# Filling the attention stacks in two halves of eight heads, each half with a semaphore of its own

## The chip, the cores and the metric

The kernel runs on one core of one Trainium2 chip. The metric is the device time of one execution in microseconds (us); the time of a kernel is the median of its runs. Five engines work side by side, each on a list of instructions of its own that it takes strictly in order: PE (matrix products), DVE (element-wise work and reductions), ACT (activations), POOL (element-wise work, memsets), and SP, which here only issues the copies that the DMA engines carry out. They wait for each other through semaphores.

## The reference

Four small transformer layers in a row, on a batch of 4 with 256 tokens of 128 channels and 16 heads. Layer 0 has heads of 64 channels, layer 1 is a graph attention over 20 nodes, layers 2 and 3 have heads of 8 channels. The attentions of layers 2 and 3 are what the change touches:

```python
# layer 2
energy = jnp.einsum('bhqd,bhkd->bhqk', q, k)
att = jax.nn.softmax(energy, axis=-1) / D ** 0.5
out = jnp.einsum('bhqk,bhkd->bhqd', att, v)
...
# layer 3
scores = jnp.einsum('bhqd,bhkd->bhqk', q, k) * scale
scores = jnp.where(causal, scores, -jnp.inf)
attn = jax.nn.softmax(scores, axis=-1)
out = jnp.einsum('bhqk,bhkd->bhqd', attn, v)
```

## The kernel before

Every batch element goes through the layers by itself, and the phases of different elements are interleaved. `schedule()` lays out once, when the program is built, which phase gets the next tick; `walk` then writes each engine's instructions in that order. So the order on every engine is fixed, and an engine that waits holds up everything behind it.

There are twelve attentions, four in each of the layers 0, 2 and 3. This document writes (2, 3) for layer 2, batch element 3. An attention has 16 heads. For a head PE first makes plain scores (`scores`, L1433 in layer 2, L1437 and L1439 in layer 3), DVE takes row maxima from them (L1131, L1128), these are turned by PE (L1462), copied by ACT (L953) and spread by POOL (L767), and six steps after the plain scores PE makes the transposed scores (`scores_t`, L1479 and L1481). ACT takes their exponentials (L961) and PE multiplies them with the values (`values`, L1527). The tail of one attention overlaps the head of the next.

In layers 2 and 3 a query or a key of 8 channels is split into three bf16 parts. PE multiplies the queries' and keys' projections (`qkv`, L1707), ACT and DVE split them (L1039, L1336, L1045, L852), and for one attention SP writes six blocks of 64 KB into the DRAM tensor `scratch` (L721). From there copies fill the *stack*: 72 rows of queries and 72 rows of keys for each head, so that one product of 72 rows forms all nine products of parts. There are two rooms for stacks, `b % ROOMS`; the rooms are slices of the tensor `big`. One fill is six copies of 192 KB:

- three copies for the queries (L731), each the three-fold repetition of one part over 24 rows, 8 KB in a row;
- three copies for the keys (L736), each all three parts over 24 rows, 8 KB in a row.

A fill of room r for the third and later attentions of these layers may begin only when the attention that used the room two before has made its 16th transposed scores (L727, semaphore `st_full`). For the first two, where layer 0 used the room, the copies wait for memsets by POOL (`stack_zero`). All copies of all fills count on one semaphore, `stack_ready`; PE waits once, ahead of an attention's first plain scores, until it shows that all six copies of its fill have landed (L1543). SP also waits for it before it overwrites `scratch` (L717).

Of the kernel before, what the change touches and what calls it, by code (L numbers as in the profile page):

```python
# [14 lines left out]
B, T, D = 4, 256, 128  # L15
ROOMS = 2
H_ROOMS = 3
NT = T // 128
H = 16
DH0 = 64  # L20
DH = D // H
# [51 lines left out]
PARTS = 3  # L73
COPIES = PARTS * DH
# [13 lines left out]
ATTENTIONS = [(layer, b) for layer in (0, 2, 3) for b in range(B)]  # L88
# [30 lines left out]
U_BASE = {a: H * n for n, a in enumerate(ATTENTIONS)}  # L119
# [124 lines left out]
def score_heads(layer, i):  # L244

    if layer != 0:
        return [i] if i < H else []
    return [i, i + 1] if i < H and i % 2 == 0 else []
# [10 lines left out]
def mT_step(layer, i):  # L259

    return next((g for g in range(GROUPS) if mT_step_of(layer, g) == i), None)
# [18 lines left out]
def x_after(*phase):  # L280
    return X_UPDATES.index(phase) + 1
# [102 lines left out]
def cond_seq_kernel(nc, x_t, adj, w0, wqk0, w1, w2, w3, wp2, wproj3, vecs, rows, out_t):  # L384
    with ExitStack() as ctx:
# [3 lines left out]
        def sem(name):  # L389
            return ctx.enter_context(nc.semaphore(name))  # L390
# [37 lines left out]
        stacks = big[:, :, :].bitcast(BF16).rearrange("p r (s h t) -> p r s h t", s=2, h=H)  # L428
# [47 lines left out]
        scratch = nc.dram_tensor("scratch", [ROOMS, 2, PARTS, DH, H * T], BF16).ap()  # L476
# [25 lines left out]
        with nc.Block() as block:  # L502
            @block.sync
            def _(sp):

                mod0 = slice(*W0_AT["mod"])
                sp.dma_start(vec[:], vecs).then_inc(first_in, 16)
                sp.dma_start(w0s[:, mod0], w0[:, mod0]).then_inc(first_in, 16)
                sp.dma_start(xT[:, 0, :], x_t[0]).then_inc(x_loaded[0], 16)
                for s in range(2):  # L510
                    sp.dma_start(wqk0s[s * DH0:(s + 1) * DH0], wqk0[:, s]).then_inc(wqk_in, 16)
                for b in range(1, B):
                    sp.dma_start(xT[:, b, :], x_t[b]).then_inc(x_loaded[b], 16)
                sp.dma_start(w0s[:, mod0.stop:], w0[:, mod0.stop:]).then_inc(w0_in, 16)
                sp.dma_start(wbias[:], rows[0:1, D:D + NL + 1].broadcast_to([128, NL + 1])).then_inc(wbias_in, 16)
                sp.dma_start(w1s[:], w1).then_inc(weights_in, 16)
                sp.dma_start(w2s[:], w2).then_inc(weights_in, 16)
                sp.dma_start(w3s[:], w3).then_inc(weights_in, 16)
                sp.dma_start(bv2[:], rows[0:1, 0:D].broadcast_to([128, D])).then_inc(weights_in, 16)
# [92 lines left out]
        part_in_dram = [sem(f"part{p}_in_dram") for p in range(PARTS)]  # L612
        stack_zero = sem("stack_zero")
        stack_sel = sem("stack_sel")
        stack_ready = sem("stack_ready")

        s_full = sem("s_full")
        max_done = sem("max_done")
# [6 lines left out]
        st_full = sem("st_full")  # L625
# [66 lines left out]
        with nc.Block() as block:  # L692
            @block.sync
            def _(sp):

                for b in range(B):
                    if b >= ROOMS:

                        sp.wait_ge(cond_step, 7 * (b - ROOMS) + 4)
                    for n in range(NT):  # L700
                        nodes = slice(n * 128, (n + 1) * 128)
                        sp.dma_start(adj_s[:, b % ROOMS, 0, n, :].rearrange("p (m l) -> p m l", l=NL),
                                     adj[b, nodes, 0:NG, :]).then_inc(adj_loaded[b], 16)
                        sp.dma_start(adj_s[:, b % ROOMS, 1, n, :].rearrange("p (m l) -> p m l", l=NL),
                                     adj[b, 0:NG, nodes, :].rearrange("m p l -> p m l")).then_inc(adj_loaded[b], 16)

                sp.wait_ge(pads_zero, 2)
                for src, dst in ((wp2, wpad[2]), (wproj3, wpad[3])):
                    by_j = src.rearrange("(g j d) n -> j d g n", g=4, j=4)
                    for j in range(4):  # L710
                        sp.dma_start(dst[32 * j:32 * j + DH, :, :], by_j[j]).then_inc(pads_in, 16)

                for a, (_, layer, b) in enumerate(QKVS):
                    r = b % ROOMS
                    if a >= ROOMS:

                        sp.wait_ge(stack_ready, 16 * 2 * PARTS * (a - ROOMS + 1))  # L717
                    for p in range(PARTS):
                        sp.wait_ge((part1_ready, part2_ready, part3_ready)[p], (2, 1, 1)[p] * (a + 1))
                        for s in range(2):  # L720
                            sp.dma_start(scratch[r, s, p].rearrange("d (h t) -> h d t", h=H), parts[:, r, p, s]  # L721
                                         ).then_inc(part_in_dram[p], 16)

                    if a < ROOMS:
                        sp.wait_ge(stack_zero, 4 * a + 2)
                    else:
                        sp.wait_ge(st_full, U_BASE[ATTENTIONS[B + a - ROOMS]] + H)  # L727
                    for p in range(PARTS):
                        sp.wait_ge(part_in_dram[p], 16 * 2 * (a + 1))
                        copies = scratch[r, 0, p].unsqueeze(0).broadcast_to([PARTS, DH, H * T])  # L730
                        sp.dma_start(stacks[COPIES * p:COPIES * (p + 1), r, 0].rearrange("c h t -> c (h t)"), copies  # L731
                                     ).then_inc(stack_ready, 16)
                    if a < ROOMS:
                        sp.wait_ge(stack_zero, 4 * a + 4)
                    for o in range(PARTS):
                        sp.dma_start(stacks[COPIES * o:COPIES * (o + 1), r, 1].rearrange("c h t -> c (h t)"),  # L736
                                     scratch[r, 1].rearrange("p d n -> (p d) n")).then_inc(stack_ready, 16)
                for b in range(B):
                    sp.wait_ge(x_ready, x_after("mlp", 3, b))
                    sp.dma_start(out_t[b], xT[:, b, :]).then_inc(out_stored, 16)  # L740
                sp.wait_ge(out_stored, 16 * B)
# [619 lines left out]
            def _(pe):  # L1361
# [54 lines left out]
                def attention(layer, b):  # L1416
                    hpo = HEADS_PER_O[layer]
                    if layer != 0:
                        a = QKVS.index(("qkv", layer, b))
# [23 lines left out]
                    def score_pair(pair):  # L1443

                        pe.wait_ge(gb_ready, H // 2 * b + pair[0] // 2 + 1)
                        for h in pair:
                            wait_s_bank_free(pe, "s", u_base + h)
                        for q in range(NT):
                            for h in pair:
                                half = slice(DH0 * (h % 2), DH0 * (h % 2 + 1))  # L1450
                                ins = nc.tensor.matmul(s_bank("s", u_base + h)[:, q * T:(q + 1) * T],
                                                       qk0b[half, b % ROOMS, h // 2, 0, q * 128:(q + 1) * 128],
                                                       qk0b[half, b % ROOMS, h // 2, 1, :], start=True, stop=True)
                                if q == NT - 1:
                                    ins.then_inc(s_full, 1)
# [84 lines left out]
                                             ).then_inc(pt_used, 1)  # L1540

                    if layer != 0:
                        pe.wait_ge(stack_ready, 16 * 2 * PARTS * (a + 1))  # L1543
                        pe.wait_ge(stack_sel, GROUPS * min(a + 1, ROOMS))
                    for i in range(STEPS):
                        heads = score_heads(layer, i)
                        if len(heads) == 2:
                            score_pair(heads)
                        elif heads:
                            scores(i)  # L1550
                        g = mT_step(layer, i)
                        if g is not None and layer == 0:
                            shift_rows(g)
                        yield
                        if g is not None and layer != 0:
                            shift_rows(g)
                        heads = turned_heads(layer, i)
                        if len(heads) == 2:
                            turned_pair(heads)
                        elif heads:  # L1560
                            scores_t(i - ST_LAG)
                        n = PV_GROUP[layer]
                        if 0 <= i - PV_LAG < H and (i - PV_LAG) % n == n - 1:
                            values(range(i - PV_LAG - n + 1, i - PV_LAG + 1))
                        yield
# [213 lines left out]
```

## Time and profile before

| | |
|---|---|
| time, median of 3 runs | 522.18 us (520.29 to 524.02) |
| the profiled execution's own time | 519.42 us |
| its span, from the first to the last instruction | 517.7 us |
| PE busy | 416.6 us, 80% of the span |
| DVE busy | 310.0 us, 60% |
| ACT busy | 281.7 us, 54% |
| POOL busy | 175.4 us, 34% |
| mean granted clock of PE | 0.954 of 2.4 GHz |

Busy time is the time in which an engine executes an instruction. In a timeline row the number in square brackets is the idle time of the engine just before that instruction, and behind the arrow stands what ended it. `DMA share` in a table of windows is the mean busy share of the core's 16 DMA engines, `PEclk` the granted clock as a share of 2.4 GHz (1.00 is 2.4 GHz, 0.50 is 1.2 GHz).

### The profile page before, as it was taken

The page shows a single profiled execution, that of the slowest core. Times are in us where ns is not written, and L with a number is a line of the kernel's source. Part 1 is how long each engine was busy: PE and PEld are TensorE (multiplying, and loading weights), DVE is VectorE, ACT ScalarE, POOL GpSimd, SP SyncE. Part 2 cuts the span into 40 slices and gives each one's busy share as a digit, 9 for nine tenths or more (in the row PEclk, how much of TensorE's full clock was granted, in tenths as well). Part 3 has the DMA queues.
Part 4 walks back from the last instruction along what each step waited for, and adds up shares of the span by engine and source line. Part 5 has one row for each costly group of instructions (what it writes and reads, how often), then busy time and mean ns, then how long its engine had stood idle before and what let it go on. Part 6 is the DMA issues. An engine that isn't in the chain of part 4 may idle for free. (4 is left out here: it accounts for less than half of the span.)

```text
span 517.7 us, 9289 instructions
## 1 busy us (share of the span) xinstructions
PE 416.6 (80%) x3196; PEld 265.1 (51%) x3196; DVE 310.0 (60%) x846; ACT 281.7 (54%) x597; POOL 175.4 (34%) x226
## 2 busy tenths in 40 slices
PE   2868687988889988889969798874785879699975
PEld 2634454555546555455636464442444656476653
DVE  2464776764574456734675758584694777656821
ACT  2243354465553744637556674564464666578774
POOL 2802221231263422864396215333031332312200
PEclk9998999999999999999989898698797999899998
DMA  8920033000000000110012130003041303130000
GB/s 230 250 23 1 2 35 46 1 1 1 0 1 2 1 1 26 59 40 2 1 61 62 32 92 2 2 17 99 11 98 36 95 27 100 43 101 13 3 11 10
DMA packets 33014, 21.24 MB, mean 41 GB/s; under 512 B 22472, under 2 KB 31048, under 8 KB 31432
## 3 DMA queue, kind: packets, MB, share of 16 engines
q1 hardware_dynamic: 32968, 20.65, 16.0%
q8 instruction: 26, 0.43, 0.4%
q14 instruction: 20, 0.16, 0.1%
HBM read 16.97 MB, written 3.67 MB: 40 GB/s over the span
## 5 line engine op out<-in xcount | busy, mean ns | idle before, releaser
L961 ACT ACTIVATE pt<-psum 128x512 f32<-128x512 f32 (+1 forms) x192 | 106.0, 558 | 101.8 <-PE psum L1503 46.1
L1131 DVE TENSOR_REDUCE negm<-psum 128x2 f32<-128x512 f32 x128 | 84.6, 683 | 45.2 <-PE psum L1433 31.8
L756 POOL TENSOR_TENSOR pairsum<-pt 128x256 f32<-128x256 f32 x64 | 46.7, 730 | 141.2 <-ACT pt L961 137.8
L767 POOL COPY big<-mT 32x1024 bf16<-32x1024 bf16 x32 | 33.1, 1035 | 135.5 <-ACT mT L953 135.2
L1479 PE MATMUL psum<-big 128*128 128x256 bf16 (+1 forms) x256 | 52.5, 276 | 4.0 <-POOL big L767 2.8
L1128 DVE TENSOR_REDUCE negm<-psum 128x3 f32<-128x384 f32 x64 | 34.8, 555 | 25.2 <-PE psum L1439 24.5
L1498 PE MATMUL psum<-big 64*128 64x256 f32 x256 | 39.2, 397 | 2.4 <-ACT pt L961 2.3
L1172 DVE TENSOR_TENSOR oT<-psum,rden 128x256 f32<-128x256 f32 x64 | 26.5, 414 | 17.2 <-ACT rden L977 16.6
L1402 PE MATMUL psum<-hT,pt 128*128 128x256 f32 x128 | 34.6, 408 | 2.1 <-DVE negm L1131 1.2
L1437 PE MATMUL psum<-big 72*128 72x128 bf16 (+1 forms) x128 | 26.3, 257 | 12.3 <-DMA big<-scratch 8.8
L1527 PE MATMUL psum<-pt,room 128*64 128x256 f32 x256 | 35.4, 399 | 0.0
L1433 PE MATMUL psum<-big 72*128 72x256 bf16 x128 | 27.1, 297 | 10.0 <-DMA big<-scratch 8.2
L1527 PE MATMUL psum<-pt,vpad 128*32 128x256 f32 (+1 forms) x512 | 33.2, 380 | 1.6 <-DVE oT L1172 1.6
L1107 DVE COPY big<-psum 128x512 f32<-128x512 f32 x32 | 22.0, 689 | 20.1 <-PE psum L1402 19.9
L1479 PEld LDWEIGHTS psum<-big 128*128 128x128 bf16 x256 | 24.9, 103 | 14.2 <-issue 5.4
L1058 DVE SCALAR_TENSOR_TENSOR xT<-psum,mods_all,xb 128x256 f32<-128x256 f32 x20 | 9.7, 483 | 35.9 <-PE psum L1596 18.7
L1402 PEld LDWEIGHTS psum<-hT,pt 128*128 128x128 f32 x128 | 23.6, 198 | 10.7 <-issue 4.1
L841 POOL TENSOR_SCALAR xb<-xT,mods_all 128x256 f32<-128x256 f32 x24 | 22.2, 928 | 17.8 <-DVE xT L1058 16.5
L929 ACT CAST room<-big 128x512 bf16<-128x512 f32 x32 | 19.1, 612 | 14.3 <-DVE big L1107 14.2
L1498 PEld LDWEIGHTS psum<-big 64*128 64x128 f32 x256 | 19.5, 186 | 12.8 <-ACT pt L961 5.5
L1439 PE MATMUL psum<-mask_qk,identb 128*128 128x128 bf16 x128 | 25.9, 226 | 0.0
L977 ACT ACTIVATE rden<-rden,zero 128x256 f32<-128x256 f32 x48 | 24.4, 508 | 1.6
(184 smaller groups left out, 863.7 us busy)
## 6 DMA issues: line engine op xcount, KB each, us to landing
big<-scratch SPq DMA_DIRECT2D x48, 192.0 KB
scratch<-room SPq DMA_DIRECT2D x48, 64.0 KB, 2.0
adj_s<-adj SPq DMA_DIRECT2D x16, 110.0 KB, 3.7
w0s<-w SPq DMA_DIRECT2D x1, 1536.0 KB, 11.2
w3s<-w SPq DMA_DIRECT2D x1, 1088.0 KB, 12.1
room<-wqk SPq DMA_DIRECT2D x2, 512.0 KB, 7.9
xT<-x_t SPq DMA_DIRECT2D x4, 128.0 KB, 8.0
w1s<-w SPq DMA_DIRECT2D x1, 512.0 KB, 10.2
```

Of the source, the lines that this page charges most:

```text
L756: nc.gpsimd.tensor_tensor(pairsum[:, u % SUM_RING, :], pt[:, pt_slot(u), 0:T], pt[:, pt_slot(u), T:2 * T], ALU.add).then_inc(pairsum_ready, 1)
L767: nc.gpsimd.tensor_copy(stacks[SHIFT_ROW:128, b % ROOMS, 0, GH * g:GH * (g + 1), :], mT[SHIFT_ROW:128, at % 2, :].unsqueeze(1).broadcast_t ...
L961: nc.scalar.activation(pt[:, pt_slot(u), 0:width], psum[:, ST_BANK + u % 2, 0:width], ACT.Exp, scale=EXP_SCALE[layer]).then_inc(pt_ready, 1)
L1128: ins = nc.vector.tensor_reduce(negm[:, g, :, j], bk[:, 0:384].rearrange("p (n k) -> p n k", n=NT + 1), AX_X, ALU.max, negate=True)
L1131: ins = nc.vector.tensor_reduce(negm[:, g, 0:NT, j], bk.rearrange("p (q k) -> p q k", q=NT), AX_X, ALU.max, negate=True)
L1172: nc.vector.tensor_tensor(oT[:, b % ROOMS, c, :], psum[:, O_BANK + o % 2, 0:T], rden[:, o % 2, :], ALU.mult).then_inc(o_done, 1)
L1402: ins = nc.tensor.matmul(s_bank("G", n, b)[:, s * T:(s + 1) * T], wqk0t[:, s, 128 * n:128 * (n + 1)], hT0[:, b % H_ROOMS], start=True, sto ...
L1433: ins = nc.tensor.matmul(bk[:, q * T:(q + 1) * T], lhs, keys, start=True, stop=True)
L1437: nc.tensor.matmul(bk[:, at:at + (q + 1) * 128], lhs, keys[:, 0:(q + 1) * 128], start=True, stop=False)
L1479: ins = nc.tensor.matmul(dst, lhs, rhs[:, q0:T], start=True, stop=(layer == 2))
L1498: nc.tensor.matmul(psum[:, ST_BANK + h % 2, k * T:(k + 1) * T], qk0[half, b % ROOMS, h // 2, 1, k * 128:(k + 1) * 128], qk0[half, b % ROOM ...
L1527: ins = nc.tensor.matmul(bk[at:at + m, qk:T], lhs, pt[:, pt_slot(u_base + h), k * T:(k + 1) * T - qk], start=(k == 0), stop=(k == NT - 1))
```

## The change

A fill is made in two halves: heads 0 to 7, then heads 8 to 15. Each half is again three copies for the queries and three for the keys, now with 4 KB in a row, 96 KB a copy. Each half of each room has a semaphore of its own. PE waits for the first half ahead of the attention's first plain scores and for the second half ahead of the ninth head's. On SP the first half waits for the 8th transposed scores of the room's previous user, the second half for the 16th. For the first two fills both waits on POOL's memsets stand in the first half, and the second half repeats them.

```diff
-        stack_ready = sem("stack_ready")
+        stack_ready = [[sem(f"stack{r}_half{half}_ready") for half in range(2)] for r in range(ROOMS)]
...
-                        sp.wait_ge(stack_ready, 16 * 2 * PARTS * (a - ROOMS + 1))
+                        for half in range(2):
+                            sp.wait_ge(stack_ready[r][half], 16 * 2 * PARTS * (a // ROOMS))
...
-                    if a < ROOMS:
-                        sp.wait_ge(stack_zero, 4 * a + 2)
-                    else:
-                        sp.wait_ge(st_full, U_BASE[ATTENTIONS[B + a - ROOMS]] + H)
-                    for p in range(PARTS):
-                        sp.wait_ge(part_in_dram[p], 16 * 2 * (a + 1))
-                        copies = scratch[r, 0, p].unsqueeze(0).broadcast_to([PARTS, DH, H * T])
-                        sp.dma_start(stacks[COPIES * p:COPIES * (p + 1), r, 0].rearrange("c h t -> c (h t)"), copies
-                                     ).then_inc(stack_ready, 16)
-                    if a < ROOMS:
-                        sp.wait_ge(stack_zero, 4 * a + 4)
-                    for o in range(PARTS):
-                        sp.dma_start(stacks[COPIES * o:COPIES * (o + 1), r, 1].rearrange("c h t -> c (h t)"),
-                                     scratch[r, 1].rearrange("p d n -> (p d) n")).then_inc(stack_ready, 16)
+                    for half in range(2):
+                        heads, at = slice(half * H // 2, (half + 1) * H // 2), half * H * T // 2
+                        if a < ROOMS:
+                            sp.wait_ge(stack_zero, 4 * a + 2)
+                        else:
+                            sp.wait_ge(st_full, U_BASE[ATTENTIONS[B + a - ROOMS]] + (half + 1) * H // 2)
+                        for p in range(PARTS):
+                            sp.wait_ge(part_in_dram[p], 16 * 2 * (a + 1))
+                            copies = scratch[r, 0, p, :, at:at + H * T // 2].unsqueeze(0).broadcast_to([PARTS, DH, H * T // 2])
+                            sp.dma_start(stacks[COPIES * p:COPIES * (p + 1), r, 0, heads].rearrange("c h t -> c (h t)"), copies
+                                         ).then_inc(stack_ready[r][half], 16)
+                        if a < ROOMS:
+                            sp.wait_ge(stack_zero, 4 * a + 4)
+                        for o in range(PARTS):
+                            sp.dma_start(stacks[COPIES * o:COPIES * (o + 1), r, 1, heads].rearrange("c h t -> c (h t)"),
+                                         scratch[r, 1, :, :, at:at + H * T // 2].rearrange("p d n -> (p d) n")
+                                         ).then_inc(stack_ready[r][half], 16)
...
-                        pe.wait_ge(stack_ready, 16 * 2 * PARTS * (a + 1))
+                        pe.wait_ge(stack_ready[a % ROOMS][0], 16 * 2 * PARTS * (a // ROOMS + 1))
                         pe.wait_ge(stack_sel, GROUPS * min(a + 1, ROOMS))
                     for i in range(STEPS):
+                        if i == H // 2 and layer != 0:
+                            pe.wait_ge(stack_ready[a % ROOMS][1], 16 * 2 * PARTS * (a // ROOMS + 1))
```

On SP this is the fill for attention (2, 3) before, with the semaphores that an instruction waits for; `24x4096` is the destination, 24 rows of 4096 bf16 elements:

```order
L731 DMA big<-scratch 24x1x4096 [waits part0_in_dram,st_full]
L731 DMA big<-scratch 24x1x4096 [waits part1_in_dram]
L731 DMA big<-scratch 24x1x4096 [waits part2_in_dram]
L736 DMA big<-scratch 24x4096 x3
L721 DMA scratch<-room 16x8x256 [waits part1_ready,stack_ready]
```

And the same place of the changed program, whose lines have moved (L731 is L734, L736 is L739, L721 is L722):

```order
L734 DMA big<-scratch 24x1x2048 [waits part0_in_dram,st_full]
L734 DMA big<-scratch 24x1x2048 [waits part1_in_dram]
L734 DMA big<-scratch 24x1x2048 [waits part2_in_dram]
L739 DMA big<-scratch 24x2048 x3
L734 DMA big<-scratch 24x1x2048 [waits part0_in_dram,st_full]
L734 DMA big<-scratch 24x1x2048 [waits part1_in_dram]
L734 DMA big<-scratch 24x1x2048 [waits part2_in_dram]
L739 DMA big<-scratch 24x2048 x3
L722 DMA scratch<-room 16x8x256 [waits part1_ready,stack0_half1_ready,stack0_half0_ready]
```

Six copies became twelve, with the same number of rows each and rows half as long; nothing else stands between the two halves. On PE the order of the instructions stays the same, and only the waits differ. This is where (2, 3) starts in the changed program, at its first plain scores:

```order
L1483 MATMUL psum<-big 128x256 [waits pt_ready]
L1483 MATMUL psum<-big 128x256
L1437 MATMUL psum<-big 128x256 [waits max_done,stack_sel,stack1_half0_ready]
L1437 MATMUL psum<-big 128x256
L1378 MATMUL psum<-ident,xT 128x128 [waits x_ready]
```

and this is its ninth head, the row that has the new wait (L1437 is L1433 before, L1483 is L1479, L1602 is L1596):

```order
L1483 MATMUL psum<-big 128x256
L1602 MATMUL psum<-oT,wp2s 128x256 [waits o_done]
L1437 MATMUL psum<-big 128x256 [waits max_done,stack1_half1_ready]
L1437 MATMUL psum<-big 128x256
L1602 MATMUL psum<-oT,wp2s 128x256 [waits o_done]
```

Behind both waits stands the rest of PE's list, so a wait there holds up the previous attention's tail and the light phases too.

## Rows read from the trace of the kernel before

**Rows 1.** The waits: engine, line, waited for: us in total, times, longest.

```profile
PE psum L1437 <- DMA big<-scratch: 8.8, 3, 5.7
PE psum L1433 <- DMA big<-scratch: 8.2, 1, 8.2
SPq L731 <- PE psum L1479: 3.4, 3, 2.7
```

**Rows 2.** PE's timeline: first plain scores of (2,3), (3,0), (3,1), (3,2); start, duration.

```profile
364.27 0.61 PE L1433 MATMUL psum<-big 72*128 72x256 bf16 x2 [8.23 <-DMA big<-scratch]
...
392.81 0.29 PE L1437 MATMUL psum<-big 72*128 72x128 bf16 x1 [5.74 <-DMA big<-scratch]
...
417.71 0.23 PE L1437 MATMUL psum<-big 72*128 72x128 bf16 x1 [0.65 <-DMA big<-scratch]
...
442.95 0.23 PE L1437 MATMUL psum<-big 72*128 72x128 bf16 x1 [2.41 <-DMA big<-scratch]
```

**Rows 3.** SP's timeline: copies issued for these four fills.

```profile
345.96 4.07 SPq L721 DMA_DIRECT2D scratch<-room  x6
350.13 2.24 SPq L731 DMA_DIRECT2D big<-scratch  x3
352.42 1.64 SPq L736 DMA_DIRECT2D big<-scratch  x3
...
377.97 2.24 SPq L731 DMA_DIRECT2D big<-scratch  x3
...
402.78 2.24 SPq L731 DMA_DIRECT2D big<-scratch  x3
...
428.38 2.24 SPq L731 DMA_DIRECT2D big<-scratch  x3
```

**Rows 4.** DMA issues of the page: KB each, median us from issue to landing.

```profile
scratch<-room SPq DMA_DIRECT2D x48, 64.0 KB, 2.0
```

**Rows 5.** Windows of the fill for (2,3): busy us by engine, PEclk, DMA share, GB/s.

```profile
351.50:354.30 2.80, 2.40 (x28) 1.22 (x25) 2.77 (x10) 2.14 (x6) 1.10 (x2) 1.00 0.20 76
354.30:358.50 4.20, 1.12 (x8) 0.60 (x8) 2.21 (x8) 2.64 (x6) 1.96 (x2) 1.00 0.71 146
358.70:363.60 4.90, 0.00 (x0) 0.00 (x0) 0.00 (x0) 0.00 (x0) 0.00 (x0) 0.60 0.18 70
```

**Rows 6.** DMA queue, 347 to 351.2, then 358.7 to 363.6: packets, MB, share of 16.

```profile
q1 hardware_dynamic: 864, 0.39, 34.0%
...
q1 hardware_dynamic: 55, 0.34, 17.6%
```

**Rows 7.** PE's timeline: plain scores of the ninth head of these four attentions.

```profile
377.61 0.38 PE L1433 MATMUL psum<-big 72*128 72x256 bf16 x2
...
405.33 0.23 PE L1437 MATMUL psum<-big 72*128 72x128 bf16 x1
...
428.66 0.23 PE L1437 MATMUL psum<-big 72*128 72x128 bf16 x1
...
458.28 0.23 PE L1437 MATMUL psum<-big 72*128 72x128 bf16 x1
```

**Rows 8.** Windows behind three of the waits, then of layer 3's middle.

```profile
365.00:369.50 4.50, 4.50 (x30) 2.20 (x29) 3.02 (x9) 1.52 (x5) 0.00 (x0) 0.50 0.01 4
392.90:397.20 4.30, 4.30 (x21) 3.31 (x22) 1.91 (x5) 2.47 (x6) 1.03 (x1) 0.50 0.00 0
444.90:448.20 3.30, 3.30 (x22) 2.84 (x23) 2.17 (x7) 2.58 (x6) 2.13 (x2) 0.52 0.15 40
393.00:470.00 77.00, 65.69 (x664) 47.71 (x663) 53.27 (x167) 50.88 (x116) 20.49 (x20) 0.95 0.24 64
```

**Rows 9.** DVE's timeline: its first work after the wait of (3,0).

```profile
393.57 0.56 DVE L1128 TENSOR_REDUCE negm<-psum 128x3 f32<-128x384 f32 x1 [5.51 <-PE psum L1439]
```

**Rows 10.** SP's timeline: the copies of the keys for (2,1).

```profile
271.47 1.13 SPq L736 DMA_DIRECT2D big<-scratch  x3
```

**Rows 11.** PE's timeline: the first plain scores of (2,1).

```profile
286.25 0.39 PE L1433 MATMUL psum<-big 72*128 72x256 bf16 x2
```

## The prediction

> **What bounds the kernel now.** PE is the busiest engine, and its list is in order, so I first read what PE waits for, longest total first. Of the waits on a fill there are four, 8.8 + 8.2 = 17.0 us [rows 1]. PE's timeline then shows where they lie: all four stand at the first plain scores of an attention, (2, 3) with 8.23 us, (3, 0) with 5.74, (3, 1) with 0.65 and (3, 2) with 2.41 [rows 2]. They are the last to end there: in 358.70 to 363.60 us not one engine has an instruction, only the DMA engines work [rows 5]. What stands still there is the whole chip, so a wait removed here is time removed, as far as the engines behind PE keep up. In layer 3's middle, 393 to 470 us, PE is busy for 65.7 of 77 us, DVE for 53.3, ACT for 50.9, POOL for 20.5 [rows 8]: PE is nearest to its limit and the others have room.
>
> SP's timeline gives the length of a fill. For (2, 3) the first copy is issued at 350.13 and PE goes on at 364.27: 14.1 us [rows 2, 3]. For the other three it is 392.81 - 377.97 = 14.8, 417.71 - 402.78 = 14.9 (in this one PE had hardly to wait, so it is that long indeed) and 442.95 - 428.38 = 14.6. The length hardly varies, so it is the fill's own. SP had issued all six copies 3.9 us after the first (350.13 to 354.06) [rows 3]; the rest is transfer. The windows of the DMA engines show how it goes: first 0.20 of 16 engines busy, then 0.71 of them with 146 GB/s, then for 5 us 0.18 of them with 70 GB/s [rows 5]. 0.18 of 16 is three engines. The fill ends on a tail in which three engines work through a list.
>
> **What the change removes.** The wait for the second half of the bytes. I cost a half from the trace. In the tail the packets are 8 KB: 17.6% of 16 engines for 4.9 us is 13.8 us of engine time for 0.34 MB, 40 ns a KB. The copies to DRAM ahead of it have 512-byte rows: 34.0% of 16 for 4.2 us is 22.8 us for 0.39 MB, 59 ns a KB [rows 6]. Packets of 4 KB are not in the trace; they lie between these two, and by 8 KB, to which they are nearer, half the bytes take half the time. What does not shrink is the time that a copy takes however small: 64 KB land 2.0 us after their issue [rows 4]. So of 14.1 us, 2.0 stay and 12.1 are halved: the first half lands 2.0 + 6.05 = 8.1 us after the first issue, 6.0 us ahead of the whole.
> - (2, 3): PE is ready at 364.27 - 8.23 = 356.04, 5.9 us after the first issue. It now waits 8.1 - 5.9 = 2.2 us; **6.0 us** saved. Bounds: none left, 8.2 saved; at 59 ns a KB the half would take 2 + 6.05 x 59/40 = 10.9 us, 3.2 saved.
> - (3, 0): 5.74 is under 6.0, so the wait goes; **5.7 us**. At 10.9 us a half, 3.9.
> - (3, 1) and (3, 2): **0.65** and **2.4 us**, at either price.
>
> Sum 14.8 us (10.2 to 17.0).
>
> **What it adds.** Six more issues in a fill: by their first six, 3.9 us more of SP's time. Behind them on SP stand the next fill's copies to DRAM. With the fill for (2, 3) SP ends at 354.06, with the addition near 358; the next fill begins at 377.97, and the six copies to DRAM ahead of it take some 4 us. Of these four fills each begins at least 24 us after the one before it [rows 3]. Zero, then; without that room each us would come on top of the next fill.
>
> The second wait: PE comes to the ninth head 377.61 - 364.27 = 13.3, 12.5, 11.0 and 15.3 us after the first [rows 2, 7]. The second half lands 6 us after the first half does, about when the whole did. Even with PE faster by the clock term below there is at least 3 us to spare: zero.
>
> The new start of a half after the 8th instead of the 16th transposed scores: SP waited for these three times, 3.4 us in all [rows 1], and in none of the four costly fills is it the long part (SP goes from the copies to DRAM to L731 within 0.1 us for (2, 3)) [rows 3]. I count nothing; at most the fill for (3, 1) moves ahead, and its wait is in the sum already.
>
> The first two fills now have their second half behind both memset waits. For (2, 1) that is 271.47 + 1.1 for the first half's keys, then 8.1 us as above: landed by 281, where PE comes at 286.25 [rows 10, 11]. Zero, covered by 5 us.
>
> **The clock.** After three of the waits PE's granted clock is 0.50, which is 1.2 GHz: 4.5 us behind (2, 3), 4.3 behind (3, 0), 3.3 behind (3, 2), with PE busy throughout [rows 8]. Without the wait this work could run at 2.4 GHz and take half, but not less than the busiest other engine needs in it. Behind (3, 0): 4.3 to ACT's 2.5, 1.8 us saved. Behind (3, 2): 3.3 to ACT's 2.6, 0.7. Behind (2, 3) a wait of 2.2 us stays, as long as that of (3, 2) which was followed by 3.3 us at 1.2 GHz; I save 0.4. Together 2.9 at most, nothing at least; I take 2.0, since short waits between engines will eat some.
>
> **What is given back.** When PE no longer stops at 387.07 for (3, 0), DVE is still at work until 393.57 - 5.51 = 388.06 [rows 9]: 1.0 us in which PE will run into DVE. I subtract 1.0 (up to 3 if the same happens elsewhere).
>
> **Sum:** 14.8 + 2.0 - 1.0 = 15.8 us. The profiled execution took 519.42 us, so 503.6; it is 2.8 us under the median of the runs, 522.18. Against the median: 522.18 - 15.8 = **506.4 us**.
>
> **Rivals.**
>
> *A copy has its price whatever its size* (slower). If a half's six copies take as long as the whole's six, 14.1 to 14.9 us, the four first waits stay and the second half lands 14 us later than the first, behind the ninth head's plain scores: waits of 0.8 at (2, 3), 2.3 at (3, 0), 3.9 at (3, 1), none at (3, 2), from the distances above [rows 2, 7]. That is 7.0 us on top: 529 us. It turns from gain to loss where a half takes about 13.6 us. Against it: six copies to DRAM were issued within 4.07 us and each landed in 2.0, so fixed shares overlap [rows 3, 4], and in the tail three engines are busy with bytes throughout [rows 5].
>
> A rule stands behind this rival: the Trainium skill (DMA: Bandwidth & Descriptors, Anatomy of one DMA) gives a fixed cost of about 2.0 us a copy plus bytes at 436 GB/s, for copies issued by GpSimd, and its Rules for kernel authors advise one large transfer over many small ones. Were the copies taken one after another, that would be an estimate of 6 x 2.2 = 13.3 us a half, near no gain. By the overlap in the rows just named I don't follow it here.
>
> *The halves are not served in turn* (the change does less than it says). All twelve copies go into the same queue. If the second half's query copies get in ahead of the first half's key copies on the three engines of the tail, that is 24 of the 30 rows which each of these three carries in a half, 0.8 x 6.05 = 4.8 us: the first half lands at 12.9. Then (2, 3) waits 7.0, (3, 0) 12.9 + 0.7 - 9.1 = 4.5 (its fill is 0.7 us longer, and PE comes 9.1 us after its issue), (3, 1) nothing and (3, 2) 12.9 + 0.5 - 12.2 = 1.2: 12.7 of 17.0 stay, no clock returns, 4.3 us gained: 518 us. For it: the middle window, where all is in flight at once, is the slow one per engine. Against: SP issues one half wholly ahead of the other.
>
> *The time is waited for elsewhere*. Half of the gain comes back, because the chains of maxima, exponentials and normalizations, which caught up during the four waits, now end last. 522.18 - 8 = 514 us. For it: DVE at 388.06. Against: the empty window in rows 5, and PE's 65.7 of 77 us.
>
> *All of it*: no wait stays and the whole clock term comes, 17.0 + 2.9 = 19.9: 502 us.
>
> **How the numbers follow.** The forecast, with everything from 502 to 511, 0.70; all of it or more 0.06; waited for elsewhere 0.13; not in turn 0.06; price per copy 0.05. The likeliest gives 506.4. The range runs from 500 (all of it, 2 us under for the scatter of the runs, 520.29 to 524.02) to 514.5 (half given back). A measurement tells about 1%, 5.2 us. Faster by more than that: the forecast, all of it, and nearly all of the half given back, 0.88; within 1%: not in turn, and the price per copy at its turning point, 0.08; slower 0.04.
>
> **What would show it.** Right: in PE's waits a sum on fills of 2 to 4 us, at (2, 3) alone; from SP's first copy to the first plain scores of (2, 3) some 8 us; no wait at the ninth heads; at (3, 0) a clock of 1.00 throughout; the time up to 356 us unchanged. Wrong: a packet of 4 KB that takes much more than 160 ns; a wait at the ninth head; more idle time of PE behind DVE or ACT in 356 to 500 us by as much as the fills lost.

## The result

| | before | after |
|---|---|---|
| time, median of 4 runs each on one chip | 521.23 us (518.33 to 524.02) | 502.54 us (501.76 to 503.15) |
| the profiled execution's own time | 519.42 us | 503.15 us |
| its span | 517.7 us | 501.4 us |
| PE busy | 416.6 us | 412.6 us, 82% of the span |
| mean granted clock of PE | 0.954 | 0.969 |

The ratio is 0.9641, with a 95% interval of 0.9583 to 0.9699: the changed kernel is 3.6% faster. The forecast was 506.4 us in a range of 500.0 to 514.5, so its likeliest case came, 3.9 us faster than said. Between the two profiled executions the step is 16.3 us, where the working had 15.8.

The lines of the code have moved: L1433, L1437, L1439 and L1462 of before are L1437, L1441, L1443 and L1466 now, L731 and L736 are L734 and L739. The one wait of PE on a fill that is left in the changed kernel, over the whole span (engine, line, waited for: us in total, times, longest):

```profile
PE psum L1437 <- DMA big<-scratch: 1.6, 1, 1.6
```

Of the 17.0 us on fills [rows 1] one wait of 1.6 us is left. Where it stands and what the other three attentions do is in PE's timeline of the changed kernel (start, duration, line, operation, idle time before and what ended it): the first plain scores of (2, 3), its ninth head, then the first of (3, 0) and its first turned maxima, and the first of (3, 1) and (3, 2).

```profile
358.60 0.39 PE L1437 MATMUL psum<-big 72*128 72x256 bf16 x2 [1.56 <-DMA big<-scratch]
...
370.15 0.38 PE L1437 MATMUL psum<-big 72*128 72x256 bf16 x2
...
379.56 0.23 PE L1441 MATMUL psum<-big 72*128 72x128 bf16 x1
...
380.75 0.27 PE L1466 MATMUL psum<-identb,m 128*128 128x128 bf16 x2 [0.50 <-DVE m L1162]
...
402.54 0.23 PE L1441 MATMUL psum<-big 72*128 72x128 bf16 x1
...
425.33 0.23 PE L1441 MATMUL psum<-big 72*128 72x128 bf16 x1
```

Against [rows 2] the brackets of 5.74, 0.65 and 2.41 are gone and that of 8.23 is 1.56. The ninth head of (2, 3) has no bracket either, as [rows 7] had none, and so it is with the ninth heads of the three others. SP's timeline of the same stretch:

```profile
349.50 2.24 SPq L734 DMA_DIRECT2D big<-scratch  x3
351.78 1.25 SPq L739 DMA_DIRECT2D big<-scratch  x3
353.13 2.17 SPq L734 DMA_DIRECT2D big<-scratch  x3
355.35 1.25 SPq L739 DMA_DIRECT2D big<-scratch  x3
366.36 4.06 SPq L722 DMA_DIRECT2D scratch<-room  x6
```

The twelve copies are issued in 7.1 us (349.50 to 356.60), where six took 3.9 [rows 3], and then SP stands for 9.8 us until the next fill's copies to DRAM: the added issues lie in SP's free time. PE's first products come 358.60 - 349.50 = 9.1 us after the first issue, instead of 14.1.

The windows of the changed kernel tell the rest (stretch, its length, busy us and instructions of PE, PE's weight loads, DVE, ACT and POOL, PEclk, DMA share, GB/s): a stretch ahead of the wait of (2, 3), the stretches behind the first plain scores of (2, 3) and (3, 0), two in (3, 2), and all from (2, 3) to the end.

```profile
345.00:350.00 5.00, 4.29 (x28) 2.02 (x27) 2.60 (x8) 1.94 (x4) 1.16 (x1) 0.52 0.24 66
358.60:363.00 4.40, 3.94 (x38) 2.31 (x38) 3.95 (x12) 2.52 (x6) 0.05 (x1) 1.00 0.17 70
379.60:383.90 4.30, 3.41 (x34) 2.52 (x30) 3.30 (x10) 3.35 (x8) 1.03 (x1) 1.00 0.17 70
430.00:435.00 5.00, 3.51 (x48) 2.36 (x45) 4.36 (x17) 3.41 (x10) 2.58 (x3) 1.00 0.16 44
435.00:438.70 3.70, 3.48 (x9) 2.70 (x10) 0.62 (x2) 2.58 (x5) 0.00 (x0) 0.54 0.39 120
...
358.50:501.40 142.90, 117.90 (x1160) 82.45 (x1160) 93.91 (x290) 96.56 (x212) 33.77 (x34) 0.98 0.17 51
```

And of the kernel before, the first and the last of these stretches:

```profile
345.00:350.00 5.00, 3.74 (x37) 2.42 (x35) 3.76 (x11) 2.56 (x6) 1.17 (x1) 1.00 0.19 52
...
364.20:517.70 153.50, 122.27 (x1160) 85.62 (x1160) 94.20 (x290) 96.46 (x212) 33.62 (x33) 0.94 0.17 46
```

**The balance of the two profiles.** PE is ready for (2, 3) at 358.60 - 1.56 = 357.04, 1.0 us later than before: the fill was issued 0.6 us sooner (349.50 for 350.13), and PE then took 1.6 us more, as 345 to 350 us ran at 0.52 (1.2 GHz) and not at 1.00. The wait there is 6.7 us shorter. From the first plain scores of (2, 3) to the end the same 1160 products now take 142.8 us (501.4 - 358.60) where they took 153.4 (517.7 - 364.27), 10.6 less: 8.8 us of fill waits are gone, PE's busy time fell by 4.4 (122.27 to 117.90) because more of it ran at 2.4 GHz, and its other idle time grew by 2.6 (153.5 - 122.3 - 8.8 = 22.4; 142.9 - 117.9 = 25.0). Together 1.0 - 6.7 - 8.8 - 4.4 + 2.6 = -16.3 us, the step between the spans.

The same windows from one attention's first plain scores to PE's being ready for the next show where the last two terms lie. Before, from (2, 3) to (3, 0), from (3, 0) to (3, 1) and from (3, 2) to the end:

```profile
364.27:387.07 22.80, 20.38 (x156) 11.76 (x156) 18.86 (x55) 14.54 (x33) 6.10 (x6) 0.88 0.23 55
392.81:417.06 24.25, 21.22 (x212) 14.89 (x212) 18.35 (x56) 15.13 (x34) 7.15 (x7) 0.91 0.24 66
442.95:517.70 74.75, 60.29 (x566) 44.43 (x566) 39.24 (x124) 50.84 (x106) 14.15 (x14) 0.95 0.10 28
```

And after:

```profile
358.60:379.56 20.96, 17.90 (x156) 10.41 (x157) 18.67 (x55) 14.62 (x33) 6.15 (x7) 1.00 0.25 77
379.56:402.54 22.98, 19.24 (x216) 13.33 (x213) 19.07 (x60) 15.04 (x35) 7.14 (x7) 1.00 0.28 83
425.33:501.40 76.07, 60.46 (x570) 44.20 (x566) 39.25 (x124) 51.38 (x107) 14.16 (x14) 0.96 0.10 30
```

In these three stretches PE is busy for 2.5 us less, 2.0 less and 0.2 more, and idle for 0.6, 0.7 and 1.1 us more. From (3, 1) to (3, 2) the two kernels differ by less than 0.1 us.

### The profile page after: what moved, and what is told of

Same layout as the page of the kernel before. It is cut to its first block and busy times, and to the rows that moved or that the text cites. A ratio compares the mean times of both kernels' runs of the same rounds, so it can differ in the third digit from the quotient of the medians.

```text
span 501.4 us, 9353 instructions
## 1 busy us (share of the span) xinstructions
PE 412.6 (82%) x3196; PEld 262.0 (52%) x3196; DVE 309.7 (62%) x846; ACT 281.8 (56%) x597; POOL 175.4 (35%) x226
## 3 DMA queue, kind: packets, MB, share of 16 engines
q1 hardware_dynamic: 34480, 20.65, 15.8%
## 5 line engine op out<-in xcount | busy, mean ns | idle before, releaser
L1483 PE MATMUL psum<-big 128*128 128x256 bf16 (+1 forms) x256 | 50.3, 266 | 4.6 <-POOL big L771 3.4
L1531 PE MATMUL psum<-pt,room 128*64 128x256 f32 x256 | 36.5, 408 | 0.0
L1483 PEld LDWEIGHTS psum<-big 128*128 128x128 bf16 x256 | 24.0, 100 | 14.4 <-ACT pt L965 5.4
L1437 PE MATMUL psum<-big 72*128 72x256 bf16 x128 | 25.9, 285 | 3.5 <-DVE negm L1135 1.9
L1441 PE MATMUL psum<-big 72*128 72x128 bf16 (+1 forms) x128 | 25.3, 249 | 3.5 <-DVE negm L1132 3.2
L1443 PE MATMUL psum<-mask_qk,identb 128*128 128x128 bf16 x128 | 25.0, 220 | 0.0
```

The source lines that it names most:

```text
L1437: ins = nc.tensor.matmul(bk[:, q * T:(q + 1) * T], lhs, keys, start=True, stop=True)
L1441: nc.tensor.matmul(bk[:, at:at + (q + 1) * 128], lhs, keys[:, 0:(q + 1) * 128], start=True, stop=False)
L1483: ins = nc.tensor.matmul(dst, lhs, rhs[:, q0:T], start=True, stop=(layer == 2))
L1531: ins = nc.tensor.matmul(bk[at:at + m, qk:T], lhs, pt[:, pt_slot(u_base + h), k * T:(k + 1) * T - qk], start=(k == 0), stop=(k == NT - 1))
```

## The experiments

The kernels ran in three groups, each on one chip with the kernel before beside it, which took 521.98, 520.38 and 519.92 us there; a ratio is to the one of its group. "After" is the changed kernel. The part of the program ahead of all fills that PE waits for ends earlier or later by up to 5 us from one profiled execution to the next: the first plain scores of (2, 0) start between 240.4 and 245.3 us. So I don't read differences under some 3 us between medians of two groups.

### Where the gain comes from: PE waits for both halves

First group. After, but PE waits for both halves ahead of the first plain scores; the twelve copies and the earlier refill stay.

```diff
-pe.wait_ge(stack_ready[a % ROOMS][0], 16 * 2 * PARTS * (a // ROOMS + 1))
+for half in range(2):
+    pe.wait_ge(stack_ready[a % ROOMS][half], 16 * 2 * PARTS * (a // ROOMS + 1))
...
-if i == H // 2 and layer != 0:
-    pe.wait_ge(stack_ready[a % ROOMS][1], 16 * 2 * PARTS * (a // ROOMS + 1))
```

> The changed program, but PE waits for both halves ahead of an attention's first plain scores. Theory (the gain is the wait for the second half's bytes): all of it goes, the time is that of before, 519 to 523 us, and in the trace the first plain scores of (2, 3) stand some 14 us behind SP's first copy. Rival (the gain comes from the halves' earlier refill or from the shorter rows): 502 to 506 us.

Measured: 516.46 us, ratio 0.9920 [0.9882, 0.9959]. Most of the gain is gone, but not all; it came 2.5 us under what I had expected. The rest needed a second kernel.

### The twelve copies by themselves

Second group. As above, and the refill waits for the 16th transposed scores again: what is left of the change is twelve copies for six.

```diff
-sp.wait_ge(st_full, U_BASE[ATTENTIONS[B + a - ROOMS]] + (half + 1) * H // 2)
+sp.wait_ge(st_full, U_BASE[ATTENTIONS[B + a - ROOMS]] + H)
```

> Twelve copies of half the size in a fill and nothing else: PE waits for both halves, and both halves of a refill wait for the 16th transposed scores. The run in which only PE's wait was whole came out at 516.5 us, 5.5 under before, which the theory had not expected. If the shorter copies themselves land the whole fill sooner (13.4 and 13.7 us at (2, 3) and (3, 0) there, 14.1 and 14.8 before), this one is at 515 to 518 us. If the earlier refill gave the 5.5 us, it is at 520 to 523 us.

Measured: 518.75 us, ratio 0.9944 [0.9907, 0.9981]. PE's timeline at the first plain scores of (2, 3), (3, 0) and (3, 2) (what ended the wait is put down as "issue" here: the trace names no single releaser):

```profile
364.67 0.59 PE L1437 MATMUL psum<-big 72*128 72x256 bf16 x2 [7.59 <-issue]
...
392.02 0.26 PE L1441 MATMUL psum<-big 72*128 72x128 bf16 x1 [4.57 <-issue]
...
441.71 0.22 PE L1441 MATMUL psum<-big 72*128 72x128 bf16 x1 [2.45 <-issue]
```

The three brackets sum to 14.6 us; (3, 1) has none. With 17.0 before [rows 2] the halved copies alone save 2.4 us of waits, since at three of the four fills the last of twelve lands sooner than the last of six: 13.5, 13.7, at most 14.2 (PE comes then and doesn't wait) and 14.6 us after the first issue, before 14.1, 14.8, 14.9 and 14.6. The kernel with the earlier refill shows nearly the same (13.4, 13.7, at most 14.6, 14.5; waits of 7.45, 4.58, none and 2.32), so what was left of its gain isn't shown to be the refill's. The intervals of the two overlap: they are not told apart.

### The earlier refill by itself

After, but both halves of a refill wait for the 16th transposed scores (the diff above alone). First group, then once more in the second beside after itself.

> The changed program, but both halves of a refill wait for the 16th transposed scores of the room's previous user. Theory: the earlier refill of the first half is worth nothing, 501.5 to 503.5 us. Rival (the earlier refill carries part of the gain, at (3, 1) and (3, 3), where SP waits for these scores): 504 us or more, with a wait of PE at (3, 1) or (3, 3).

> Both halves of a refill wait for the 16th transposed scores, once more, with more rounds: the first time gave 505.1 us with runs from 501.7 to 507.2. Theory (the earlier refill is worth nothing): within 1.5 us of the changed program beside it. Rival (worth some 2.5 us): 504.5 us or more while the changed program is at 502.5.

> The changed program once more, beside the two runs that it is to be compared with. 501.5 to 504 us by both theories; it fixes the level on this chip.

Measured: 505.06 us, ratio 0.9687 [0.9607, 0.9767], then 503.02, ratio 0.9655 [0.9614, 0.9696]; after beside the latter 504.05, ratio 0.9674 [0.9639, 0.9708]. The first time was above what was expected; in the repeat, beside after itself, the kernel without the earlier refill is not slower. The first profile has a fill wait of 0.36 us at (3, 0) besides that at (2, 3), the second none besides it; at (3, 1) and (3, 3), where the rival looked for one, there is none in either. That edit is worth nothing that can be measured here.

The kernel with the copies alone and this one differ in nothing but PE's waits: 518.75 and 503.02 us, in one group. **That is 15.7 of the 17.4 us which this kernel gains over the one before in its group (520.38), from one edit:** PE no longer waits for the second half ahead of the first plain scores.

### Quarters, and whether a copy has a price of its own

First group. After, with four parts of four heads: 24 copies of 48 KB in a fill, 2 KB in a row, PE waits ahead of heads 0, 4, 8 and 12.

```diff
+CUTS = 4
...
-for half in range(2):
-    heads, at = slice(half * H // 2, (half + 1) * H // 2), half * H * T // 2
+for half in range(CUTS):
+    heads, at = slice(half * H // CUTS, (half + 1) * H // CUTS), half * H * T // CUTS
...
-if i == H // 2 and layer != 0:
-    pe.wait_ge(stack_ready[a % ROOMS][1], 16 * 2 * PARTS * (a // ROOMS + 1))
+if i in (4, 8, 12) and layer != 0:
+    pe.wait_ge(stack_ready[a % ROOMS][i // 4], 16 * 2 * PARTS * (a // ROOMS + 1))
```

> The fill in four parts of four heads, each with its semaphore and its wait on PE: 24 copies a fill. Theory (bytes, not copies, set the time): the first quarter of (2, 3) lands some 5.5 us after SP's first copy, and the rest of the wait there, 1.6 us in the changed program, is gone: 500 to 502 us. Rival (a copy has its price whatever its size): the first quarter lands no earlier than the half's 9.1 us and later quarters hold PE up: 504 us or more.

Measured: 498.86 us, ratio 0.9583 [0.9508, 0.9658], 1.1 us under what I had expected. SP's first issue for (2, 3), and PE's first plain scores of it:

```profile
350.16 2.25 SPq L735 DMA_DIRECT2D big<-scratch  x3
```

```profile
355.89 0.38 PE L1438 MATMUL psum<-big 72*128 72x256 bf16 x2
```

No bracket: a quarter is there within 5.7 us of its first issue, when PE comes, and no fill wait is left in the kernel. If six copies took 14.1 us whatever their size, PE would have waited some 8 us here. The rival *a copy has its price whatever its size* falls, the copies being four times as many as before.

### The other way to a shorter fill: the same six copies over more engines

First group. The kernel before, with nothing of the change; only the order of the rows in each copy is another, the channel ahead of the repetition or the part, so that the outermost count is 8. The queries' outermost count was 3, the keys' 24; the edit changes both.

```diff
-copies = scratch[r, 0, p].unsqueeze(0).broadcast_to([PARTS, DH, H * T])
+copies = scratch[r, 0, p].unsqueeze(1).broadcast_to([DH, PARTS, H * T])
...
-scratch[r, 1].rearrange("p d n -> (p d) n")
+scratch[r, 1].rearrange("p d n -> d p n")
```

The stack's rows stand in another order within their 24, queries and keys alike, so that each product still meets its partner.

> The kernel before, with the whole fill and one wait; only the order of the 72 rows in a stack is another (channel ahead of copy), so that the queries' copies have 8 groups of rows outermost instead of 3. Theory (the end of a fill is three engines that work through a list): a fill is 18 rows of 8 KB an engine at the most instead of 30, the fill of (2, 3) takes 9 to 10.5 us instead of 14.1, and the time is 506 to 510 us. Rival (the DMA engines contend for one thing, 146 GB/s at the most, and the list is only its remainder): the fill stays above 12 us and the time above 515.

Measured: 505.28 us, ratio 0.9693 [0.9628, 0.9759], 0.7 us under what I had expected. SP's first issues for (2, 3) and (3, 0), PE's first plain scores of both, and a window of the fill for (2, 3):

```profile
348.33 2.10 SPq L731 DMA_DIRECT2D big<-scratch  x3
...
371.96 2.11 SPq L731 DMA_DIRECT2D big<-scratch  x3
```

```profile
358.25 0.61 PE L1433 MATMUL psum<-big 72*128 72x256 bf16 x2 [4.03 <-DMA big<-scratch]
...
381.91 0.23 PE L1437 MATMUL psum<-big 72*128 72x128 bf16 x1 [0.84 <-DMA big<-scratch]
```

```profile
349.80:357.50 7.70, 3.42 (x35) 1.78 (x32) 4.86 (x17) 4.68 (x11) 2.95 (x4) 0.95 0.48 155
```

The fill takes 9.9 us both times (358.25 - 348.33 and 381.91 - 371.96) instead of 14.1 and 14.8. In [rows 5] it ended on 5 us with 0.18 of 16 engines, three of them, at 70 GB/s; here 0.48 of 16, some eight, move 155 GB/s throughout, and no such tail follows (0.00 of 16 from 357.50 us to PE's start). By the forecast's count each of the three engines carried 60 rows of 4 KB in two halves, which is 30 of 8 KB; now, by the expectation's, each of eight carries 18. Twelve rows less at 40 ns a KB [rows 6] are an estimate of 3.8 us, and 4.2 were measured. So the tail came from the order of the rows. That it was the queries' three-fold repetition is what this count says; no run reordered the queries' copies alone.

The Trainium skill says the same of such a copy (DMA: Bandwidth & Descriptors, Rules for kernel authors): a leading repetition of c copies keeps the whole transfer on at most c engines. The trace agrees, with 0.18 of 16 against 0.48.

So two unrelated edits, one of which leaves the change out altogether, gain nearly the same by shortening the same four waits (17.0 us to 1.6 and to 4.9).

### Both together

Halves with that order of rows, in the second group and again in the third beside after and beside quarters with that order.

> The changed program, and besides the other order of the 72 rows (channel ahead of copy), which spreads the queries' copies over 8 groups. Theory (what is left at (2, 3) is the first half's list on three engines): a half lands 6 us or so after SP's first copy instead of 7.7 to 9.5, no fill makes PE wait, and the time is that of the quarters, 498 to 501 us. Rival (the two remedies add up, since a shorter fill also frees something else): clearly under 498 us.

> The halves over 8 groups once more, now beside the changed program with as many rounds: 5.4 us lay between their medians, where the wait at (2, 3) that went is 1 to 2 us. Theory: 1.5 to 3 us under the changed program, with the clock behind that wait. Rival (something else than that wait): 4 us or more again.

> The changed program beside these two, as their level: 501.5 to 505 us.

> Quarters and the other order of rows together. In quarters alone no fill made PE wait, so theory (PE's waits on fills are all that a fill costs): nothing more to gain, the time of the halves over 8 groups beside it, within 1.5 us. Rival (a shorter fill also helps where PE does not wait for it): 2 us or more under that.

| | group | median, us | ratio to before |
|---|---|---|---|
| halves, 8 outermost | second | 498.64 | 0.9592 [0.9544, 0.9641] |
| after | second | 504.05 | 0.9674 [0.9639, 0.9708] |
| halves, 8 outermost | third | 501.55 | 0.9640 [0.9587, 0.9692] |
| quarters, 8 outermost | third | 498.86 | 0.9622 [0.9579, 0.9666] |
| after | third | 505.75 | 0.9739 [0.9698, 0.9781] |

The order of rows is worth 5.4 and 4.2 us on top of the halves, more than the 1.5 to 3 that I had written; the rival's mark, 4 us or more again, is reached. PE still waits at (2, 3), where I had expected no wait: for 0.98 us in the second group's profile (a half landed 6.9 us after its first issue, I had said 6) and for 0.75 in the third's, against 1.94 and 2.97 of after. The shorter wait and the clock behind it are a part of the gain; how large a part stands below.

The medians of quarters and of halves, both with 8 outermost, are 2.7 us apart, past the 2 us that I had set for the rival, but their runs (497.5 to 502.5 and 496.9 to 503.1) and the intervals of their ratios overlap: not told apart. Halves and quarters with 8 outermost are thus faster than both kernels of this study, each beside after; quarters alone had no run of after beside them, and their ratio's interval overlaps that of after in the first comparison. Which of the three is fastest stays open.

The windows behind the first plain scores of (2, 3): of halves with 8 outermost in the second group,

```profile
353.30:358.00 4.70, 3.86 (x38) 2.24 (x38) 4.55 (x14) 3.15 (x8) 0.55 (x1) 1.00 0.30 94
```

of after in the second group, behind a wait of 1.94 us,

```profile
358.60:363.00 4.40, 4.40 (x33) 2.53 (x34) 3.33 (x11) 1.88 (x5) 0.00 (x0) 0.64 0.36 105
```

of after in the third, behind a wait of 2.97,

```profile
361.30:366.00 4.70, 4.70 (x30) 2.46 (x31) 2.64 (x8) 1.47 (x4) 0.00 (x0) 0.50 0.17 67
```

and of the second kernel without the earlier refill, behind 3.01:

```profile
355.60:360.00 4.40, 4.40 (x28) 2.23 (x28) 2.64 (x8) 1.48 (x4) 0.00 (x0) 0.50 0.17 68
```

In the first PE makes 38 products in 3.86 us of work, in the last 28 in 4.40. From PE's being ready for (2, 3) to the end of the span it takes before 161.7 us (517.7 - 356.04); after 144.4 and 144.2 with waits of 1.56 and 1.94, but 147.4 with 2.97; without the earlier refill 145.9 with 1.75 and 146.8 with 3.01; halves with 8 outermost 143.9 and 144.2; quarters 144.2 and with 8 outermost 143.7. So an execution of after with the longer wait pays some 3 us here: 1.0 to 1.4 in the wait, the rest at 1.2 GHz behind it. Quarters and 8 outermost have no such case in their profiles.

That is not all that the other order gains, and the rest is not explained. Of the 4.7 us between the two profiles of the second group (500.8 and 496.1 us) only 0.3 lie behind PE's being ready for (2, 3); 2.0 lie ahead of the first plain scores of (2, 0) and 2.4 between these two points. In the third group 3.2 of 4.7 us lie behind (2, 3) and 1.5 ahead of (2, 0). Nor is it only a bad case that goes: the fastest of after's 16 runs took 501.76 us, and five of the ten of halves with 8 outermost took less than 499.1.

## Why the prediction was right, step by step

**The main term held.** PE's wait for the second half of the bytes was the loss, and the pair of kernels that differ in PE's waits alone shows it: 15.7 us. Forecast were 2.2 us of wait left at (2, 3) and none at the other three; 1.56 was left, and none. The sign set for it, a sum on fills of 2 to 4 us, was missed by 0.4, on the better side.

**When the first half lands.** The formula, 2.0 us fixed and half of 12.1, gave 8.1. Measured were 9.1 in the profile of the changed kernel and 7.8 and 8.9 in its two others, 7.7 and 8.9 without the earlier refill, 8.5 in the mean: right within its scatter of 1.4 us. The price that it rested on, 4 KB at 40 ns a KB, held too. The DMA queue of the changed kernel in 359 to 362.5 us, where of a fill only 4 KB rows are left (packets by size; then packets, MB, share of 16 engines):

```profile
DMA packets 83, 0.28 MB, mean 80 GB/s; under 512 B 15, under 2 KB 15, under 8 KB 83
...
q1 hardware_dynamic: 83, 0.28, 19.5%
```

That is 0.195 x 16 x 3.5 = 10.9 us of engine time for 0.28 MB, 39 ns a KB, or 160 ns for each of the 68 packets of 4 KB; the other 15 are under 512 bytes. Still, the wait of (2, 3) came out near the forecast through two errors that cancel: the half landed 1.0 us later than said, and PE came 1.6 us later after the issue (7.5 instead of 5.9), because it had run at 1.2 GHz from 345 to 350 us (in the two other profiles of this kernel that stretch has a clock of 1.00, and PE comes 5.9 us after the issue). "The time up to 356 us unchanged" was wrong by that 1.0 us.

**What was added cost nothing.** SP's issues lay in its free time, the ninth heads wait for nothing, and the earlier refill is worth nothing, each as said. One thing was missed there: "the second half lands ... about when the whole did". It lands up to 1.1 us sooner (13.7 for 14.8), and twelve copies in place of six take 2.4 us off the waits even where PE waits for all. With the wait for the first half alone this plays no part, and why the shorter rows are sooner there is not shown. One reading was short: SP waited for the previous user's transposed scores four times and not three, the fourth time, for 2.4 us, at (3, 3), where the last of them stand on another line (L1481) than the one in [rows 1]. That fill comes after the four costly ones. In the changed kernel 0.9 us of these 5.8 are left.

**The clock was the term that was mis-sized:** forecast 2.0, at most 2.9; PE's busy time behind (2, 3) fell by 4.4 us. The step that failed is "I save 0.4" behind (2, 3), which took the 3.3 us at 1.2 GHz behind the wait of (3, 2) for what a wait of 2.2 us would leave there. Behind the 1.56 us that were left the clock stayed at 1.00, and up to (3, 0) PE's busy time fell by 2.5 us. This hangs on the execution: behind waits of 1.75 to 3.01 us at the same place other profiles have clocks of 0.64 to 0.50, nearer to what was forecast. For (3, 0) 1.8 was said, and 2.0 came. For (3, 2) 0.7 was said, and nothing came, since a new stretch at 1.2 GHz, from 435 us, took back what the old one gave. By halves, the stretches of [rows 8] give back 2.2 (of 4.5), 2.1 (of 4.3) and 1.6 (of 3.3), and the new stretch takes 1.8 (of 3.7): 4.1, near the 4.4. The limit "not less than the busiest other engine needs in it" put two terms into one: PE's busy time fell by about half of these stretches, with no such limit, and what the others still needed turned into idle time of PE, which is the next term. From the first plain scores of (2, 3) to those of (3, 0) it is now 20.96 us instead of 28.54, 7.6 less: the wait of 5.7 and 2.5 of busy time, less 0.6 of idle time.

**What is given back** was mis-sized the other way: 1.0 forecast, 2.6 measured, and not at (3, 0) alone: 1.1 of it stand behind the first plain scores of (3, 2). PE's idle time from 356 us to the end, behind DVE's maxima, was 0.9 us before,

```profile
PE psum L1462 <- DVE m L1158: 0.9, 2, 0.6
```

and in the changed kernel

```profile
PE psum L1466 <- DVE m L1162: 2.4, 4, 1.0
```

That is 1.5 of the 2.6. At (3, 0), the one place that the forecast named, it is 0.50. So clock less give-back was 1.8 where 1.0 was said; with 15.5 us of waits for 14.8, and 1.0 lost ahead of (2, 3), the sum is 16.3 for 15.8.

**Median and profile.** On its own terms the sum gave 503.6 us for the profiled execution, and 503.15 came. Taken from the median of 522.18 it gave 506.4, and 502.54 came: the profiled execution of before was 2.8 us under that median, the one of after 0.6 over its own, and the step was 0.5 larger, together the 3.9. Two more medians of the same kernel were 504.05 and 505.75, on the forecast's side. In the profiled execution beside the last (507.44 us, 4.3 more than the first) 2.8 us of the difference lie ahead of (2, 0), with a granted clock of 0.90 in its first 100 us instead of 0.98. What else moved the medians is not shown.

**The rivals.** A price per copy: refuted by 24 copies a fill with no wait. Halves not in turn: it wanted the first half at 12.9 us and 518 us; no kernel whose PE waits for the first half alone has it after 9.1. Waited for elsewhere: its mechanism is there, but with 2.6 us and not half the gain. All of it: 502 us is nearest to the median measured, but for (2, 3) not by its mechanism, since a wait of 1.6 us is left.

## What to carry to other kernels

When an engine waits for a fill, ask which bytes it needs first, and give these a semaphore of their own; cutting the copies is only worth what the consumer no longer waits for (15.7 us between waiting for both halves and for one; by the ratios 3 to 4 for halved copies without a split wait). Before cutting, look at how a transfer ends: a low and steady share of the DMA engines, three of 16 here, was the sign that the shape of the copies and not only their size made the fill long, and another order of rows gained nearly as much with no new semaphore. A stall costs more than its length, as PE's clock can fall behind it; count the stretch at 1.2 GHz as busy time that halves, and what other engines then can't follow as a term of its own.

## What the runs showed of the hardware

- The same bytes in the same six copies land in 9.9 us instead of 14.1 when the outermost count is 8 and not 3 for the queries and 24 for the keys. I had known the tail from [rows 5], but not that it was the larger lever on the fill.
- PE's granted clock behind a wait is not the same from one execution to the next: at (2, 3) 1.00 behind 1.56 us of idleness, 0.61 behind 1.75, 0.64 behind 1.94, 0.50 behind 2.97 and 3.01. The wait alone doesn't tell it: from 435 us on the changed kernel's clock is 0.54 behind a wait of 0.65 us, after 5 us (430.2 to 435.2) in which PE was busy for 3.31. In the kernel before the same products stand behind a wait of 0.65 too, after 5 us (447.85 to 452.85) with 3.87, and ran at 1.00. What decides it stays open.
- The stretch ahead of the first fill that PE waits for moved by up to 5 us between profiled executions (240.4 to 245.3 us for the first plain scores of (2, 0)). On a kernel with one core as well, a difference of half a per cent needs the two kernels in one group and a look at that stretch.
